# GpSimd waits for free ring slots two pairs at a time in a graph network's edge gather

## The reference

```python
ew = edge_attr @ edge_w + edge_b
for l in range(3):
    msg = relu(x[src] * ew)
    out = 0
    for i in range(3):                       # three kinds of edge
        h = segment_sum(msg * mask[i], dst) * inv_cnt[i]
        out = out + h @ weights[l, i]
    out = out + x @ roots[l] + biases[l]
    x = x + relu(out)
result = layernorm(x_in + x)
```

## Time and profile before

| | us |
|---|---|
| median of three runs (lowest, highest) | 3607.24 (3604.1, 3611.32) |
| the profiled execution, its own time | 3611.26 |
| its span, first to last instruction | 3609.5 |
| outside the span | 1.76 |

### The profile page before, as it was taken

One profiled execution on the slowest core, in us unless ns is written; L12 is line 12 of the kernel. 1 busy time (PEld: TensorE's weight loads), 2 busy tenths in 40 slices (PEclk: granted clock), 3 DMA queues, 4 the chain that ended last, 5 costly groups with the idle time before them and its releaser, 6 DMA issues.

```text
span 3609.5 us, 57851 instructions
## 1 busy us (share of the span) xinstructions
PE 2854.7 (79%) x17654; PEld 2646.3 (73%) x17654; DVE 2139.7 (59%) x6079; ACT 1204.2 (33%) x2542; POOL 2232.8 (62%) x2363
## 2 busy tenths in 40 slices
PE   6888887888888777878778778877877777787887
PEld 5777777777777676777777777777777777777776
DVE  5666666666666555555555555555555565656656
ACT  4555555555544322222222222222222222222222
POOL 6666666666666566666666666656666666666664
PEclk8788888898888878788888988887888888888888
DMA  6555555555555444444444444444444444444443
GB/s 171 153 158 152 156 156 158 150 158 160 152 158 158 125 133 122 125 132 122 129 129 125 131 125 131 128 126 130 123 124 126 127 127 128 129 126 127 127 128 97
DMA packets 313363, 491.03 MB, mean 136 GB/s; under 512 B 62115, under 2 KB 200030, under 8 KB 313054
## 3 DMA queue, kind: packets, MB, share of 16 engines
q0 software_dynamic: 112608, 307.65, 30.1%
q1 hardware_dynamic: 199628, 179.45, 16.9%
q10 hardware_dynamic: 818, 0.18, 0.0%
HBM read 429.61 MB, written 57.43 MB: 135 GB/s over the span
## 4 chain that ended last, share of the span: by engine, by line
PE 59%; issue 19%; DVE 11%; another core or an unknown queue 8%; DVEq 3%; DMA 0%; ACT 0%; ACTq 0%
PE bank L973 29%; PE bank L929 16%; PE bank L1018 12%; DVE acc L1195 5%; DVE xg L1369 2%; PE bank L994 1%; DVEq L1339 1%; DVEq L1195 1%; DVE t L1212 1%; DVE t L1251 1%; PE bank L965 0%; DVEq L306 0%; DVE t L1224 0%; DVE S L1154 0%
## 5 line engine op out<-in xcount | busy, mean ns | idle before, releaser
L781 POOL DMA_INDIRECT xg<-x,idx x1540 | 1466.0, 952 | 868.3 <-issue 385.0
L1369 DVE TENSOR_TENSOR xg<-xg,bank 128x512 f32<-128x512 f32 x1170 | 802.7, 686 | 1373.8 <-remote 785.5
L973 PE MATMUL bank<-S,xg 128*128 128x96 f32 x9384 | 1522.8, 313 | 101.6 <-issue 92.6
L973 PEld LDWEIGHTS bank<-S,xg 128*128 128x128 f32 x9384 | 1434.2, 228 | 150.2 <-issue 120.0
L863 ACT ACTIVATE xg<-xg 128x512 f32<-128x512 f32 x1170 | 736.8, 630 | 1855.0 <-issue 1070.1
L929 PE MATMUL bank<-wsb,at 128*128 128x256 f32 x4692 | 1008.8, 344 | 386.7 <-issue 240.9
L929 PEld LDWEIGHTS bank<-wsb,at 128*128 128x128 f32 x4692 | 772.0, 228 | 442.1 <-issue 358.1
L781 POOL DMA_INDIRECT xg<-in_x_dram,idx x782 | 741.7, 948 | 465.3 <-issue 181.4
L1195 DVE TENSOR_TENSOR acc<-acc,bank 128x192 f32 x2346 | 816.1, 348 | 46.0 <-issue 14.8
L1018 PE MATMUL bank<-W,acc 128*128 128x256 f32 (+1 forms) x1764 | 532.8, 422 | 36.0 <-issue 34.3
L1018 PEld LDWEIGHTS bank<-W,acc 128*128 128x128 f32 (+1 forms) x1764 | 399.0, 263 | 51.9 <-issue 40.1
(11 more groups left out here) (72 smaller groups left out, 613.9 us busy)
## 6 DMA issues: line engine op xcount, KB each, us to landing
at<-attr_t SPq DMA_DIRECT2D x585, 128.0 KB
attr_t<-hs SPq DMA_DIRECT2D x196, 128.0 KB
xg<-x,idx POOLq DMA_INDIRECT x1540
hs<-in_attr_q_dram SPq DMA_DIRECT2D x196, 64.0 KB
xg<-in_x_dram,idx POOLq DMA_INDIRECT x782
x<-t SPq DMA_DIRECT2D x96, 128.0 KB
xblk<-x SPq DMA_DIRECT2D x96, 128.0 KB
y<-t SPq DMA_DIRECT2D x94, 128.0 KB
```

Of the source, the lines that this page charges most:

```text
L781: eng.indirect_dma_start(out=xg[:, n % XR, :], out_offset=None, in_=rows_in, in_offset=bass.IndirectOffsetOnAxis(ap=rows_at, axis=0)).then ...
L973: last = eng.matmul(sums_bank(l, q, i)[:, 192 * i + 96 * h:192 * i + 96 * h + 96], xg[:, n % XR, 128 * h:128 * h + 128], S[:, slot(l, 2 * ...
L1369: eng.tensor_tensor(v, v, shared_bank("edges", l, q)[:, :].rearrange("p (i d) -> p i d", i=2), ALU.mult).then_inc(s_m, 1)
```

## The change

The wait of a gather is changed. Before, each gather from the 21st waited, both of a pair for the same value. Now only a gather whose number divides by four waits, and it waits until the slots of its own pair and of the next are free: of the pairs p and p + 1 (p even) it asks for the value that p + 1 asked for. The other three gathers of the four have no wait on `s_sc`. At the very end the asked pair is bounded by the last one.

```diff
             def gather(l, j):
                 n = l * NT + j
-                if n >= XR:
-                    eng.wait_ge(s_sc, collected(*divmod((n - XR) // 2, NP)))
+                Q = min(n // 2 + 1, L * NP - 1) - XR // 2
+                if n % 4 == 0 and Q >= 0:
+                    eng.wait_ge(s_sc, collected(*divmod(Q, NP)))
```

## The result

The changed kernel took 3624.56 us (median of 10 runs, 3618.97 to 3631.92). The kernel before, run beside it ten times, took 3610.07 (3604.1 to 3615.49). The ratio is 1.0040, with a 95% interval from 1.0032 to 1.0048: slower by some 14.5 us. The forecast was 3620. The profiled execution spans 3624.9 us (3626.59 by its own time) against 3609.5 (3611.26), so the two traces may be compared piece by piece.

The account below looks back on a forecast made before the run. GpSimd's stops on `s_sc` and the length of its rounds were taken to pace the kernel. 3611.3 (profiled) + 3.8 (layer 0) + 9.4 (layers 1 and 2) = 3624.5, less 4.0 for the median: 3620, range 3560 to 3675.

Parts of the forecast that it names:

- The lost pair of lead: GpSimd's remaining wait asks for one pair more (p - 9, not p - 10): 0 us, with 9.5 us to spare.
- Waits taken away: Three in four of the gathers' waits removed: 0 us by itself, since the gather's own time covers the test.
- Rounds of fours and eights: GpSimd's stops only at every fourth gather: layer 0 stays in fours, +3.8 us; layers 1 and 2 mix, +9.4.
- Between the two I take them in turn: Layers 1 and 2: a four follows each eight, 18.08 us for twelve gathers, 1.507 for one, +9.4 us.
- The price of a stop: GpSimd's round length: near 1.43 us for each gather and 0.45 for each stop, giving 6.17, 9.03 and 11.89.
- The other signs: Profile after: idle over 0.4 us only before every fourth gather; 1.5 and 2.0 us idle; multiply 0.13 us ahead.
- The ends: Gathers at the layers' ends wait for stores (14.34 us) and not for slots: 0 us.
- Eights: Layers 1 and 2: the check after four gathers is passed almost always, the next fails; -18 us, 3589; chance 0.27.
- Fours everywhere: Layers 1 and 2: GpSimd stops after four gathers, as in layer 0; +38 to +75 us, 3645 to 3682; chance 0.20.
- Long rounds: GpSimd's own waits hold `s_sc` back, so few stops are left; 3538, or 3465 in all layers; chance 0.08.
- Nothing: TensorE's own pace ends the stops, so GpSimd's grouping changes nothing anyone waits for; 3607; chance 0.12.
- The reading that the gathers' backlog holds `s_sc` back: Each gather costs some 1.43 us behind its visible 1.25; a stop on `s_sc` ends when that backlog is worked off.

Follow-up runs that it names:

- the fourth experiment: The kernel before, with GpSimd's gathers waiting on `s_acc` (VectorE's sums) instead of TensorE's `s_sc`: 3972.48 us, ratio 1.0983.

## Why the prediction was right, and where it was not

**Size and sign held:** 3624.56 against 3620, slower by more than 0.2% as the largest of the three chances had it, and the profiled execution 3626.6 against 3624.5.

**The lost pair of lead costs nothing:** shown, by the earlier question on every pair (0.9984). The bound of 9.0 us for the landing was loose: by the packets it is 2.5 us here, so the spare was larger than stated.

**Waits taken away cost nothing:** shown where GpSimd never stops (1.0002).

**Rounds of fours and eights:** in layers 1 and 2 the forms are as forecast, no six and near even numbers, and the two terms came out as +2.9 for +3.8 and +8.5 for +9.4. The step under them, "Between the two I take them in turn", is borne out in part. A check that fails after four because an eight left TensorE behind is seen: 48 of the 61 stops whose value was made that moment are of this kind. But it is not the rule. A four follows an eight in 24 of 25 cases in layer 0, in 38 of 61 in layer 2 and in only 23 of 67 in layer 1, where eighteen eights follow each other from 1352.87 to 1568.46 us. The even numbers do not come from a turn, and the +8.5 is made of +6.8 in layer 1 and +1.8 in layer 2, though the mix of rounds is nearly the same. Layer 0, forecast to go on in fours alone, has 25 eights, and its +2.9 comes of fours of 6.24 us and eights of 12.14: right in number only.

**The price of a stop** failed as a rule. "1.43 us for each gather and 0.45 for each stop" was fitted to rounds of the kernel before, whose values are nearly all made in time (3 exceptions in 455). It does not say what grouping does. Applied to the counts of layer 1, with its 5 twos at 3.31 us, it gives 1135.4 / 754 = 1.506 us for a gather before, and (53 x 6.17 + 68 x 11.89) / 756 = 1.502 after, a gain; the same rounds measured 1.500 and 1.509. Both sides miss: the fours of before lasted 5.86 us and not 6.17, and the eights of after 11.97 and not 11.89. That is some 10 us in the change of one layer. The prediction named a sign for this, a round of a given number of gathers with another length than before, and it came: in layer 1 a four went from 5.86 to 6.16, in layer 0 groups of three took sixes from 9.14 to 9.27. In layer 0 eighteen fewer stops (165 for 183) brought nothing, and groups of three brought nothing either. What replaces it: when GpSimd may stop only at coarse places, it sends longer bursts and then longer pauses, TensorE waits more for VectorE's multiply (336.7 us in place of 137.8), and 61 stops in place of 3 end with a value made that moment. That part is read from five traces and fits all of them, the three groupings of 1.0032 to 1.0054 and the two kernels without one; it was not varied by itself, so it is likely and not shown. With errors of this size in the rule, the agreement of the sum is in good part luck.

**The other signs.** No stop but at every fourth gather, apart from the layers' starts: held. Idle times of 1.5 and 2.0 us after fours and eights: 1.45 and 2.21 in the median. VectorE's multiply 0.13 us ahead of the gather that ends a stop: so at 95% of the stops before, at only 56% after. Where it is not so, the two engines no longer wait for one event.

**The ends** were put at 0 and cost 4.5 us: 3.1 behind the last gather and 1.4 in one passage. No run tells why; the tail may hang on where the last group happens to fall.

**The rivals.** *Eights*: not the rule; with 130 eights to 119 fours layers 1 and 2 gained nothing. *Fours everywhere*: not even layer 0, which has 25 eights. *Long rounds*: its cause falls by the fourth experiment. *Nothing*: wrong here, right on the chips where GpSimd never stops.

**The reading that the gathers' backlog holds `s_sc` back** is wrong in one part and open in the rest. That the value comes late to every engine is shown, also where GpSimd does not ask for it. A backlog of transfers is ruled out: a gather's rows land 2.5 us behind its start wherever it stands in a round. That gathers delay TensorE's value in some other way is not shown; the same program has no such waits on three other chips, and the experiments that would have told weren't run on a chip of the first kind.

## What to carry to other kernels

If an engine may stop only at every second place, its rounds can have fewer lengths: here the round of six is gone, and the mix of four and eight that replaces it is no better. Fewer waits are no gain where the waits left out never waited, and fewer stops are none where something else holds the pace, as layer 0 shows (1.544 us a gather in fours or sixes). Test such a pace rule on a second grouping before trusting its sum, and look whether the value that ends a stop was made long before or only then. Before putting a late value down to a queue of transfers, look at the packets and at the records of the semaphore itself.

## What was not expected of the hardware

The same program takes 3610 us on some chips and 2967 on others, 1.217 times. The page of the changed kernel on one of the latter:

```profile
span 2969.0 us, 57851 instructions
PE 2560.1 (86%) x17654; PEld 2403.1 (81%) x17654; DVE 2155.8 (73%) x6079; ACT 1195.0 (40%) x2542; POOL 2231.3 (75%) x2363
```

GpSimd is busy as long on both (2231.3 and 2235.6 us), VectorE and ScalarE within 1.2%, while TensorE's busy time is 258 us shorter. Its mean granted clock is 0.923 there and 0.851 here. The clock and the idle time of TensorE go together, and which is the cause these runs do not tell. On the chips of 2967 us the gathers follow each other 1.25 us apart with hardly a stop, and from the first one's start to the last one's pass 2944.8 of the 2969.0 us. On the chip of 3610 us `s_sc` is seen by VectorE, ScalarE and GpSimd late, at the start of the program 9.3 us after the collect's recorded end (24.87 to 34.16). The traces differ in one more thing: those taken where the kernel before takes 3610 us hold 18,500 to 20,600 semaphore updates, those taken where it takes 2967 hold 69,000 to 73,000. Whether this has to do with the late value, nothing here tells. The loss of this change was seen only on a chip of the first kind.
